# Attention over graph nodes with 12 heads: the broadcasts of v as products over 32 rows, issued in pairs

## What is computed

```
h      = x @ W                       (per head, 512 x 32)
th     = tanh(h)
s, d   = th @ w_src, th @ w_dst      (512 each, per head)
attn   = softmax(where(adj, leaky_relu(s_i + d_j, 0.2), -999))
feat   = elu(attn @ h + b)
gate   = sigmoid(x @ H_w.T + H_b)
out    = layernorm(x + gate * feat + (1 - gate) * x)
```

## Time and profile before

| | |
|---|---|
| time, median of 3 runs | 760.92 us (760.79 to 760.95) |
| the profiled execution | 760.79 us, span of its instructions 759.0 us |
| TensorE busy | 705.2 us, 93% of the span |
| VectorE busy | 685.7 us, 90% |
| GpSimd busy | 593.2 us, 78% |
| ScalarE busy | 376.0 us, 50% |
| mean granted TensorE clock | 0.977 of full speed |
| chain that ended last | 87% TensorE: `attend` (L824) 47%, products (L748) 26%, broadcasts (L810) 6% |

### The profile page before, as it was taken

One profiled execution on the slowest core, in us unless ns is written; L12 is line 12 of the kernel. 1 busy time (PEld: TensorE's weight loads), 2 busy tenths in 40 slices (PEclk: granted clock), 3 DMA queues, 4 the chain that ended last, 5 costly groups with the idle time before them and its releaser, 6 DMA issues.

```text
span 759.0 us, 12678 instructions
## 1 busy us (share of the span) xinstructions
PE 705.2 (93%) x3472; PEld 399.4 (53%) x3472; DVE 685.7 (90%) x1281; ACT 376.0 (50%) x804; POOL 593.2 (78%) x437
## 2 busy tenths in 40 slices
PE   4599999999999999999999999999999999999970
PEld 4365655546565554656555464655546465563430
DVE  8778989999898989999898999989899998989875
ACT  4223446274554727455462746547274654727162
POOL 6973697988979798897979889797988979793500
PEclk9699999999999999999999999999999999999995
DMA  5200111212121121113112121211312121111102
GB/s 181 97 1 2 56 42 42 74 47 76 43 97 41 41 76 47 70 41 97 41 41 84 44 65 41 97 41 41 88 45 61 41 97 41 47 51 42 41 2 83
DMA packets 32875, 43.82 MB, mean 58 GB/s; under 512 B 1234, under 2 KB 26580, under 8 KB 32852
## 3 DMA queue, kind: packets, MB, share of 16 engines
q1 hardware_dynamic: 24660, 31.35, 13.2%
q10 hardware_dynamic: 8192, 12.19, 4.4%
HBM read 30.95 MB, written 12.58 MB: 57 GB/s over the span
## 4 chain that ended last, share of the span: by engine, by line
PE 87%; DVE 5%; ACT 4%; issue 2%; DMA 1%; SPq 0%; ACTq 0%; POOL 0%; POOLq 0%; DVEq 0%
PE out_T L824 47%; PE hg L748 26%; PE vb L810 6%; PE tr L832 5%; ACT x_plus L415 2%; PE hg L795 1%; DVE ew L610 1%; DMA ew<-in_HwT 1%; ACT h_sb L381 1%; DVE th_w L541 1%; PE hg L800 1%; ACT th L380 1%; DVE ex L702 1%; DVE sd L559 1%; DMA out<-y 0%
## 5 line engine op out<-in xcount | busy, mean ns | idle before, releaser
L610 DVE SCALAR_TENSOR_TENSOR ew<-vb,u,adj_in 128x512 f32<-128x512 f32 x768 | 534.4, 742 | 2.2 <-PE vb L810 2.2
L824 PE MATMUL out_T<-ew,vals 128*64 128x512 f32 x1536 | 374.2, 601 | 1.4 <-DVE ew L610 1.3
L824 PEld LDWEIGHTS out_T<-ew,vals 128*64 128x64 f32 x1536 | 113.0, 136 | 205.7 <-issue 133.8
L258 POOL TENSOR_TENSOR th_w<-th,score_w 128x768 f32<-128x768 f32 x60 | 126.8, 2113 | 81.8 <-ACT th L380 68.6
L410 ACT ACTIVATE att_T<-out_T,tiny 128x512 f32<-128x512 f32 x96 | 66.1, 689 | 227.2 <-PE out_T L824 227.2
L748 PE MATMUL hg<-w_hi,xT_hi 128*128 128x384 f32 x384 | 110.0, 395 | 17.0 <-ACT h_sb L381 9.3
L748 PE MATMUL hg<-w_hi,xT_lo 128*128 128x384 f32 x384 | 88.9, 339 | 0.3 <-DVE xT_lo L526 0.3
L748 PE MATMUL hg<-w_lo,xT_hi 128*128 128x384 f32 x384 | 88.8, 339 | 0.0
L748 PEld LDWEIGHTS hg<-w_hi,xT_hi 128*128 128x128 f32 x384 | 70.3, 194 | 26.7 <-issue 22.8
L387 ACT ACTIVATE gate_tanh<-hg 128x384 f32<-128x384 f32 x64 | 31.5, 491 | 84.1 <-PE hg L748 84.1
L810 PE MATMUL vb<-v_T,head_sel 128*128 128x512 bf16 x192 | 71.9, 389 | 0.7 <-ACT v_T L402 0.7
(11 more groups left out here) (97 smaller groups left out, 753.4 us busy)
## 6 DMA issues: line engine op xcount, KB each, us to landing
xT_in<-in_xT SPq DMA_DIRECT2D x16, 768.0 KB, 4.6
x_in<-in_x SPq DMA_DIRECT2D x16, 768.0 KB, 4.5
out<-y ACTq DMA_DIRECT2D x15, 768.0 KB, 3.5
adj_in<-in_adjT SPq DMA_DIRECT2D x16, 256.0 KB, 4.8
ew<-in_W SPq DMA_DIRECT2D x1, 576.0 KB, 4.1
ew<-in_HwT SPq DMA_DIRECT2D x1, 576.0 KB, 7.8
score_w<-in_w_rows SPq DMA_DIRECT2D x1, 384.0 KB, 6.9
out<-y SPq DMA_DIRECT2D x1, 384.0 KB, 2.5
```

The source lines that it names most:

```text
L258: g.tensor_tensor(th_w[:, c % 2], th[:, c].unsqueeze(1).broadcast_to([P, 2, D]), score_w[:], ALU.mult).then_inc(S["thw_done"], 1)
L610: ve.scalar_tensor_tensor(out=ew[:, (2 * C * j + i) % SLOTS, :], in0=VB[h % 4][:], scalar=u[:, q, c, h:h + 1], in1=adj_in[:, q, c, :], op0 ...
L824: te.matmul(OUT[VW * k:VW * k + VW, :], vals[:, q, c, h, :], ew[:, t % SLOTS, :], start=(c == 0), stop=(c == C - 1)).then_inc(S["ew_free"], 1)
```

## The change

The three parts of head h = 4i+g are put in columns 32g+3k+i of `v_parts` in place of column 12k+h: four groups of 32 rows of v_T, of which nine count. The broadcast of head h is then a product over the 32 rows of its group h % 4 alone. ScalarE's write of the first part and VectorE's three small operations of `split_v` get access patterns that follow the new order, as do the three `affine_select` that build `head_sel`. In TensorE's program the second broadcast of each group is issued directly behind the first, ahead of the products and transposes that stood between them. No wait is added or removed.

```diff
@@ sbuf
         v_parts = sb("v_parts", [P, C, P], BF16)
+        v_part = [v_parts[:].rearrange("p c (g r) -> p c r g", g=4)[:, :, HQ * k:HQ * k + HQ, :] for k in range(NPART)]
@@
+        def by_quarter(ap):
+            return ap.rearrange("p c (i g) -> p c i g", g=4)
@@ gpsimd
                 for k in range(NPART):
-                    g.affine_select(out=head_sel[:], in_=head_sel[:], compare_op=ALU.not_equal, fill=1.0,
-                                    base=-H * k, pattern=[[-1, H], [0, P]],
+                    sel = head_sel[:].rearrange("p (i g) n -> p i g n", g=4)
+                    g.affine_select(out=sel, in_=sel, compare_op=ALU.not_equal, fill=1.0,
+                                    base=-HQ * k, pattern=[[-1, HQ], [-P // 4, 4], [0, P]],
                                     channel_multiplier=1).then_inc(S["pool_setup"], 1)
@@ scalar
-                a.activation(v_parts[:, :, 0:H], s_pos[:], ACT.Exp, scale=ALPHA - 1).then_inc(S["exps_done"], 1)
+                a.activation(v_part[0], by_quarter(s_pos[:]), ACT.Exp, scale=ALPHA - 1).then_inc(S["exps_done"], 1)
@@ vector
-                    ve.tensor_tensor(v_rest, v, v_parts[:, :, 0:H], ALU.subtract).then_inc(S["scores"], 1)
+                    ve.tensor_tensor(by_quarter(v_rest), by_quarter(v), v_part[0], ALU.subtract).then_inc(S["scores"], 1)
@@
-                    ve.tensor_copy(v_parts[:, :, H:2 * H], v_rest).then_inc(S["scores"], 1)
+                    ve.tensor_copy(v_part[1], by_quarter(v_rest)).then_inc(S["scores"], 1)
@@
-                    ve.tensor_tensor(v_parts[:, :, 2 * H:3 * H], v_rest, v_parts[:, :, H:2 * H],
-                                     ALU.subtract).then_inc(S["scores"], 1)
+                    ve.tensor_tensor(v_part[2], by_quarter(v_rest), v_part[1], ALU.subtract).then_inc(S["scores"], 1)
@@ tensor
-                te.matmul(VB[h % 4][:], head_sel[:, h], v_T[:, q], start=True, stop=True).then_inc(S["vb_ready"], 1)
+                rows = slice(P // 4 * (h % 4), P // 4 * (h % 4) + P // 4)
+                te.matmul(VB[h % 4][:], head_sel[rows, h], v_T[rows, q], start=True, stop=True).then_inc(S["vb_ready"], 1)
@@ step, group 0; groups 1 to 4 in the same way
                 broadcast_v(b, q, 2)
+                broadcast_v(b, q, 3)
                 if not last:
                     features(b + 1, 1 - q, 0)
                 if not first:
                     transpose_out(b - 1, HP - 1)
-                broadcast_v(b, q, 3)
                 if not last:
                     features(b + 1, 1 - q, 1)
                 attend(b, q, 0)
```

More of the change, by code:

```diff
@@ L36, in gat_layernorm @@
     HP = H // 2
+    HQ = H // 4
     VW = 64
@@ L848, in step @@
                 broadcast_v(b, q, 4)
+                broadcast_v(b, q, 5)
                 if not last:
@@ L851, in step @@
                 transpose_out(b, 0)
-                broadcast_v(b, q, 5)
                 if not last:
@@ L857, in step @@
                 broadcast_v(b, q, 6)
+                broadcast_v(b, q, 7)
                 gates(b, q, 0, last)
                 transpose_out(b, 1)
-                broadcast_v(b, q, 7)
                 gates(b, q, 1, last)
@@ L864, in step @@
                 broadcast_v(b, q, 8)
+                broadcast_v(b, q, 9)
                 if not last:
@@ L870, in step @@
                 transpose_out(b, 2)
-                broadcast_v(b, q, 9)
                 attend(b, q, 3)
                 broadcast_v(b, q, 10)
+                broadcast_v(b, q, 11)
                 gates(b, q, 3, last)
                 transpose_out(b, 3)
-                broadcast_v(b, q, 11)
                 attend(b, q, 4)
```

## The result

| | before | after |
|---|---|---|
| median | 760.93 us (760.79 to 763.77, 4 runs) | 769.46 us (767.87 to 770.77, 4 runs) |
| the profiled execution | 760.79 us, span 759.0 | 769.05 us, span 767.2 |

The ratio is 1.0101, 95% interval 1.0081 to 1.0122: slower by 7.7 us by this ratio (6.2 to 9.3), by 8.5 us between the two medians. The direction was forecast, the size was not: 763.7 us was predicted, with 768.5 us as the upper end of the range.

A forecast was written before the change was run, and what follows sets the result against it. TensorE was taken to bound only stage 3 and parts of 1 and 4, ScalarE and VectorE chains the rest. Per step 0.16 + 0.02 + 0.02 - 0.01 = 0.19 us, times 15 2.8: 763.7 us; range from the second rival (757.8) to 768.5.

The forecast's parts named there:

- The reading of the six stages: Period cut at its six `attend` ends: only stage 3, stage 1's last part and stage 4 up to the transposes follow TensorE.
- Pair side by side: Two broadcasts over 32 rows on TensorE run at once: 0.23 us taken, bounds 0.22 and 0.44.
- no overlap: Rival: something orders the pair's two broadcasts, which take 0.44 us; 11.7 us slower, 772.5 us; chance 0.09.
- Price of the switch: TensorE behind the pair, 32 to 128 rows: 0.20 us into features and gates, 0.15 into `max_T`, 0.14 into `attend`.
- The second rival: Rows tiled without a drain: stage 3 gains 0.21 us, 3.0 us faster in all, 757.8 us; chance 0.20.
- the case that price and gain even out: Rival: a partial switch price near 0.1 us leaves the time at 760.8 us; chance 0.11.
- the sign named for it: Timeline behind the pair: next product's first matmul 0.35 us or more later if the switch is priced, 0.23 if free.
- Stage 4: Fourth `attend`-to-`attend` stretch: pair and switch delay the transposes VectorE awaits; loss 0.16 us, bounds 0 and 0.36.
- Stage 3: Third stretch, TensorE's: 0.44 us of broadcasts become 0.43 with the switch; gain 0.01 us, bounds +0.22 and -0.21.
- Stage 1: First stretch: first product done 0.21 us later, with 0.29 us to spare before ScalarE's tanh; loss 0.02 us, 0 to 0.3.
- Small operations: Five strided bf16 patterns, ScalarE's and VectorE's on stage 5's chain: 0.02 us for all, bounds 0 and 0.15.
- Range: Whole kernel: from the second rival at the lower end up to the main case's 768.5 us.

The follow-up runs named there:

- e5: Kernel before, with head 8's broadcast moved behind the transposes of stage 4, next to head 9's: 762.24 us against 761.84, ratio 1.0009.
- e4: Changed kernel's products over 32 rows, each alone in the old order of the kernel before, with dense small operations: 772.44 us against 761.85.
- e3: Kernel before, with the second broadcast directly behind the first, both over 128 rows: 766.83 us, ratio 1.0075.
- e6: Kernel before, with heads 8 and 9 as a 32-row pair behind stage 4's transposes and 0 and 1 as a pair in stage 6: 761.49 us against 761.85.
- e2: Changed kernel with the dense small operations of the kernel before, TensorE's new program kept: 766.3 us against 761.84, ratio 1.0062.
- e9: Changed kernel, with ScalarE's first part written dense into its own tile and the strided copy behind it: 765.23 us.
- e1: Changed kernel with TensorE's old program, broadcasts over 128 rows in the old order, new layout kept: 766.46 us against 761.84, ratio 1.007.

## Why the prediction was right in direction and wrong in size

- **Bounds.** The reading of the six stages held throughout: stages 2, 3 and 6 didn't move by more than 0.02 us in any kernel that was expected to leave them alone, stage 4 shrank when the transposes came earlier (e5), and e4 moved stage 3 by the sum of its switches.
- **Pair side by side**: 0.23 us was taken, the two start 3 ns apart. Right; no overlap is refuted.
- **Price of the switch**: 0.20 us into features, taken from the switch between column widths. Right (e4: 0.49 for three switches against 0.50). The second rival, a free switch, is refuted, and with it the case that price and gain even out. Only the sign named for it was off: the next matmul was to start 0.35 us or more behind the pair and started at 0.32, as part of the price shows behind that start. That the price is one drain and what is left of a weight load is the prediction's reading; the sizes fit it (0.10 into a broadcast, 0.20 into gates), and no run separates the two. The Trainium skill (TensorEngine Tiling (Array Packing), Key Properties) states that changing the tiling mode drains TensorE; for a change of rows e4's trace agrees, with 0.10 us ahead of the broadcast.
- **Stage 4**: +0.16 forecast, +0.18 measured. Right, and e3, e5 and e6 show the mechanism from three sides. The direction was no luck: TensorE's new program alone costs 0.20 us per period (e2), where 0.17 was forecast.
- **Stage 3**: no gain, as forecast. **Stage 1**: +0.02 forecast, +0.03 measured.
- **Small operations**: this is the step that failed. 0.02 us was taken for all of them, with 0.15 as the upper bound, because the elements stay the same. They cost 0.22 us per period, nearly all of it by ScalarE's one write (e9). The term was mis-sized by a factor of ten and its bound was too low: the count of elements was read, the count of separate pieces written was not. No row of before showed a strided bf16 write, so the bound had no row behind it. (Of the five edits that were counted, four run in each batch, and one of these writes dense fp32; `affine_select` runs once, took 5.88 us for 5.85, and held up nothing.) With 0.22 the sum is 0.39 us per step, 5.9 us, and 766.8 us for the median.
- **What stood outside the sum.** The prediction gave the last step to VectorE and put it at nothing, and it has no term for the small operations at the start. In the last step and behind it TensorE's new program costs 0.45 us (64.6 and 64.7 us from the last step's first `attend` to the end in the kernel after, e2 and e3; 64.2 before and in e1). With the 6.7 us of the 15 periods that is 7.2 us, inside the measured difference, for which the interval gives 6.2 to 9.3. At the start the same small operations stand on the path once: from VectorE's first `d_rel` to the transposes of v it takes 2.06 us before and in e3, and 2.57 after and in e1. From these transposes to the first `attend` the execution after is 0.5 us shorter; four broadcasts run at once there, but TensorE's clock also falls and rises in this stretch at another time in each execution, so how much of the start belongs to the change stays open. The collision above accounts for the other 1.1 us between the two profiled executions; as it goes by when the clock rose, it is not the change's.
- **Range**: the upper end, 0.5 us per step, came from a slower pair and full prices of the switch. The term that was 0.20 us too low per step, 3.0 us in 15, is more than the 1 us by which the time lies above it.

## What to carry to other kernels

A change of data layout can be paid where the data is written: for a bf16 write to SBUF count the separate pieces, not the elements alone, and look who waits for that operation, even if it lasts 0.2 us. Two products over fewer rows, side by side, took the time of one, and the change of the array's shape ate the gain; they pay where they stand next to a switch that is paid anyway, and behind the work on which another engine waits. When an engine is 93% busy, ask for each stretch which wait ends last: only stage 3 was TensorE's alone here, and in stage 4 the order of TensorE's work mattered more than its amount.

## What the runs showed of the hardware

- A write of 48 bf16 elements per partition to SBUF in 48 pieces took 0.43 us on ScalarE and 0.36 on VectorE, in 16 pieces of three 0.28 and 0.22 to 0.25, in dense runs of twelve 0.24 and 0.20. An fp32 write to PSUM on VectorE took 0.22 us in 48 pieces and dense.
- A switch of the array between 32 and 128 rows cost 0.10 us into a bf16 broadcast and 0.20 us into an fp32 product of gates, the prices taken from switches between 64 and 128 columns.
- An earlier rise of TensorE's clock (at 11.3 to 12.3 us in place of 13.3 to 14.8) went with scores that were ready 1.1 us later, in 11 of 11 executions, by way of a collision between GpSimd and VectorE in which an operation of 0.96 us took 3.5.
